# A graph attention layer on one core: the split of the next h moved ahead of the tile's last combine, a simpler row bias, and one more block of each tile transposed on TensorE

## The reference

```python
h = jnp.maximum(_layernorm(x, axis=-1), 0.0)
scores = jnp.einsum('nd,md->nm', h, ks)
scores = jax.nn.leaky_relu(scores, negative_slope=0.2)
scores = jnp.where(adj > 0, scores, NEG_BIG)
attn = jax.nn.softmax(scores, axis=1)
x = x + jnp.einsum('nm,md->nd', attn, ks)
```

## Time and profile before

| | |
|---|---|
| Median of three runs | 1803.49 us |
| The profiled execution | 1804.0 us |
| Its span | 1802.2 us |
| Mean granted TensorE clock | 0.994 |
| TensorE matmul busy | 1617.3 us, 90% |
| ScalarE busy | 1606.0 us, 89% |
| VectorE busy | 1564.4 us, 87% |
| GpSimd busy | 750.0 us, 42% |

### The profile page before, as it was taken

How to read it: one execution, slowest core, us unless ns; L and a number is a source line. 1 busy time by engine, 2 the same in 40 slices (tenths; PEclk the granted TensorE clock), 3 DMA queues, 4 the chain that set the end, 5 groups by cost and what they waited for, 6 DMA issues and landing times. The chain is left out here.

```text
span 1802.2 us, 37484 instructions
## 1 busy us (share of the span) xinstructions
PE 1617.3 (90%) x13442; PEld 1185.6 (66%) x13442; DVE 1564.4 (87%) x2592; ACT 1606.0 (89%) x2081; POOL 750.0 (42%) x713
## 2 busy tenths in 40 slices
PE   5799898898898898898898998988988988989988
PEld 3466666676666676666676666666766666666666
DVE  7888898898888888888888888988988888888885
ACT  7798898898898898898898988988988988989988
POOL 1344344443443443443443443444434434434433
PEclk9899999999999999999999999999999999999999
DMA  7699999999999999999999999999999999999996
GB/s 216 189 241 232 243 237 242 244 230 242 240 237 239 238 241 235 245 239 234 245 232 242 241 234 243 234 237 250 231 242 245 227 245 238 221 246 242 234 246 125
DMA packets 613686, 421.91 MB, mean 234 GB/s; under 512 B 547968, under 2 KB 580736, under 8 KB 580736
## 3 DMA queue, kind: packets, MB, share of 16 engines
q1 hardware_dynamic: 613504, 419.53, 97.7%
HBM read 281.02 MB, written 4.19 MB: 158 GB/s over the span
## 5 line engine op out<-in xcount | busy, mean ns | idle before, releaser
L322 POOL TENSOR_TENSOR halves<-scores,halves 128x512 f16<-128x512 f32 x512 | 596.5, 1165 | 995.0 <-ACT halves L485 995.0
L607 DVE CUSTOM_DVE_ANT_0 scores<-ps_scores,mask,minus_scale 128x1024 f32<-128x1024 f32 x512 | 654.8, 1279 | 3.3 <-PE ps_scores L370 2.7
L468 ACT ACTIVATE scores<-scores,neg_max 128x1024 f32<-128x1024 f32 x512 | 582.3, 1137 | 0.0
L461 ACT ACTIVATE scores<-scores 128x1024 f32<-128x1024 f32 x512 | 537.6, 1050 | 9.8 <-DVE pair_min L607 9.7
L368 PE MATMUL ps_scores<-keysT_hi,hT_hi 128*128 128x512 f16 x1024 | 390.2, 381 | 166.3 <-DVE hT_lo L536 154.1
L616 DVE TENSOR_TENSOR probsT_lo<-ps_T,probsT_hi 128x512 f16<-128x512 f32 x512 | 351.8, 687 | 192.2 <-ACT probsT_hi L476 192.0
L476 ACT ACTIVATE probsT_hi<-ps_T 128x512 f16<-128x512 f32 x512 | 305.6, 597 | 167.5 <-PE ps_T L379 161.9
L394 PE MATMUL ps_out<-keys,probsT_hi 128*128 128x258 f16 x2048 | 399.6, 274 | 6.3 <-issue 4.5
L370 PE MATMUL ps_scores<-keysT_hi,hT_lo 128*128 128x512 f16 x1024 | 390.4, 381 | 0.0
L589 DVE TENSOR_SCALAR mask<-adj_in 128x2048 bf16<-128x2048 int32 x256 | 390.1, 1524 | 0.1
L369 PE MATMUL ps_scores<-keysT_lo,hT_hi 128*128 128x512 f16 x1024 | 390.0, 381 | 0.0
(11 more groups left out here) (52 smaller groups left out, 749.1 us busy)
## 6 DMA issues: line engine op xcount, KB each, us to landing
adj_in<-in_adj_dram SPq DMA_DIRECT2D x256, 1024.0 KB, 5.6
turned<-halves SPq DMA_TRANSPOSE x512, 6.0
x_in<-in_x_dram SPq DMA_DIRECT2D x64, 64.0 KB, 5.3
keys_in<-in_L_gnn_ks_dram SPq DMA_DIRECT2D x8, 512.0 KB, 7.3
x_res<-in_x_dram SPq DMA_DIRECT2D x64, 64.0 KB, 4.9
out_dram<-out_tile SPq DMA_DIRECT2D x64, 64.0 KB, 5.3
```

Source lines behind the costliest of these rows:

```text
L322: nc.gpsimd.tensor_tensor(half[:, BLOCK:2 * BLOCK], probs(t, b), half[:, 0:BLOCK], ALU.subtract) \
L461: nc.scalar.activation(s, s, ACT.Prelu, alpha=1.0 / SLOPE).then_inc(leaky_ready, 1)
L468: nc.scalar.activation(s, s, ACT.Exp, bias=neg_max[:, t % 2:t % 2 + 1], scale=-SLOPE) \
L607: nc.vector.tensor_tensor_reduce(out=score_pair(q, p), in0=ps_scores[:, slots, :].rearrange("p s k -> p (s k)"), in1=mask[:, (p // 2) % 2, ...
```

## The change

There are four edits.

1. `split_h` moves on VectorE from step 15, where it stood behind the last combine and `minimum`, to step 14 ahead of the last combine. So that its input is there, `transpose_h` moves on TensorE from step 13 to step 12, `weigh` and `finish` on VectorE from step 11 to step 10 (there ahead of the combine of pair 5), and the store of the tile and the load of the residual on SyncE from step 13 to step 11.
2. The row bias loses an instruction. Before, an amount of 9.7 was added only where the maximum was small, which took a comparison (L637) and a multiply-add (L643). Now 7.99 is always added.
3. Block 15 leaves `BY_DMA`. Its high half is then made on ScalarE from PSUM in step 3, its low half on VectorE in step 3, it is transposed on TensorE in step 3 and multiplied in step 5. Seven blocks of a tile stay with the DMA.
4. Functions for a variant with the high half on VectorE, which had no blocks, are gone.

```diff
-    BY_DMA = tuple(b for b in range(BLOCKS) if b % 2 == 1)
+    BY_DMA = tuple(b for b in range(BLOCKS) if b % 2 == 1 and b != 15)
...
-    LIFT = 14 * 0.6931471805599453
-    LIFT_BELOW = 2.0 ** 22
+    LIFT = 7.99
...
-                    if j == 13 and prev:
+                    if j == 11 and prev:
                         store(i - 1)
...
-                    if j == 13 and ahead:
+                    if j == 12 and ahead:
                         transpose_h(i + 2, odd)
...
-                nc.vector.tensor_scalar(lift[:, :], plain_max[:, :], plain_max[:, 0:1], LIFT_BELOW ** 2,
-                                        ALU.mult, ALU.is_lt) \
-                    .then_inc(lift_ready, 1)
-                dve.wait_ge(lift_ready, q + 1)
                 if q > 1:
                     dve.wait_ge(probs_ready, (q - 1) * PAIRS)
-                nc.vector.scalar_tensor_tensor(out=neg_max[:, q % 2:q % 2 + 1], in0=lift[:, :], scalar=LIFT,
-                                               in1=plain_max[:, :], op0=ALU.mult, op1=ALU.add) \
+                nc.vector.tensor_scalar(neg_max[:, q % 2:q % 2 + 1], plain_max[:, :], LIFT, None, ALU.add) \
                     .then_inc(neg_max_ready, 1)
...
-                        if j == 15:
+                        if j == 14:
                             split_h(i + 2, odd)
-                    if prev and j == 11:
+                    if prev and j == 10:
                         weigh(i - 1, 1 - odd)
                         finish(i - 1, 1 - odd)
```

More of the change, by code:

```diff
@@ L38, in gat_kernel @@
     HI_LAG = 2
-    HI_DVE_LAG = 3
     LO_LAG = 3
@@ L42, in gat_kernel @@
     ADD_LAG = 10
-    BY_DMA = tuple(b for b in range(BLOCKS) if b % 2 == 1)
+    BY_DMA = tuple(b for b in range(BLOCKS) if b % 2 == 1 and b != 15)
     BY_PE = tuple(b for b in range(BLOCKS) if b not in BY_DMA)
-    HI_ON_DVE = tuple(b for b in BY_DMA if False)
-    HI_ON_ACT = tuple(b for b in BY_DMA if b not in HI_ON_DVE)
     EPS = 1e-5
@@ L109, in gat_kernel @@
         plain_max = sbuf("plain_max", [P, 1], fp32)
-        lift = sbuf("lift", [P, 1], fp32)
         neg_max = sbuf("neg_max", [P, 2], fp32)
@@ L152, in gat_kernel @@
         plain_max_ready = sem("plain_max_ready")
-        lift_ready = sem("lift_ready")
         neg_max_ready = sem("neg_max_ready")
@@ L161, in gat_kernel @@
         half_hi_ready = sem("half_hi_ready")
-        half_hi_dve_ready = sem("half_hi_dve_ready")
         half_lo_ready = sem("half_lo_ready")
@@ L190, in nth_pe @@
             return t * len(BY_PE) + sum(c < b for c in BY_PE)
[L192 to L196, removed]
         def nth_dma(t, b):
@@ L316, in split_half_lo @@
                 n = nth_dma(t, b)
[L317 to L320, removed]
+                pool.wait_ge(half_hi_ready, n + 1)
                 half = halves[:, n % R_SLOTS, :]
@@ L508, in step @@
                         split_keys_hi(j // 2)
-                    split = behind(i, j, HI_LAG, HI_ON_ACT, this, prev)
+                    split = behind(i, j, HI_LAG, BY_DMA, this, prev)
                     if split:
@@ L617, in split_probs_lo @@
                                         ALU.subtract).then_inc(T_lo_ready, 1)
[L619 to L625, removed]
             def minimum(q):
@@ L689, in step @@
                         split_probs_lo(*split)
-                    split = behind(i, j, HI_DVE_LAG, HI_ON_DVE, this, prev)
-                    if split:
-                        split_half_hi(*split)
                     if ahead:
```

## The result

The changed kernel takes 1710.54 us, the median of four runs (1709.86 to 1711.83); the kernel before took 1803.15 beside it. The ratio is 0.9481, with a 95% interval of 0.9463 to 0.9499. The number lies in the predicted range of 1668 to 1720, outside the 1682 to 1702 of the forecast case. One step of the mechanism was wrong: a part of the stop for hT stayed, and the new wait in step 2 did not come.

What follows compares the result with a forecast made beforehand. TensorE's pace inside a tile plus its stop for hT bounds the kernel: 1802.2 - 161.3 (stop) + 27.7 (block 15) + 22.7 (new wait) - 1.0 (end) = 1690.3, plus 1.8 around it: 1692 us; forecast 1682 to 1702, range 1668 to 1720.

Steps and rivals of the forecast that it cites:

- forecast case: The main expectation for the changed kernel: 1692 us, within 1682 to 1702; chance 0.47.
- stop for hT: TensorE waits once per tile, before step 0, for `hT_lo`; removing it was to save 2.56 us a tile.
- new wait in step 2: TensorE would wait in step 2 for `probsT_lo` of block 12; 0.36 us a tile.
- My own loop: Walk through TensorE, ScalarE and VectorE from block 12's output in step 2 back to it; about 25.5 to 25.7 us.
- pairs 6 and 7: Score banks TensorE needs in steps 0 and 2; ready near 20.3 and 23.1, needed at 21.0 and 24.1, so neither decides.
- The loop's size: Tile time of the walked loop, taken as 25.55 us, a wait of 0.36 above TensorE's 25.19.
- held loop: Rival: GpSimd's block 13 meets L633 or the mask, or ScalarE's pair waits add up; 26.0 us a tile, 1718 us; chance 0.22.
- predicted 27.7: Cost in us of block 15's four transposes on TensorE, 0.44 us a tile over 63 tiles.
- The DMAs: Transposes queued behind a 1 MB adjacency load were to keep their margin, 8.0 to 8.8 us; priced at nothing.
- Late turned blocks: Rival: the four blocks behind an adjacency load land late for TensorE; 1843 us at 9.2 us landings; chance 0.03.
- the stop only moved by half: Rival: `transpose_h` in step 12 waits for `finish`, or the first score bank is late; half of 2.56 us returns, 1774 us; chance 0.07.
- no effect: Rival: hT isn't there in time and TensorE's stop stays; 1832 us; chance 0.01.

Runs made afterwards that it cites:

- best: Changed kernel with block 15 back on the DMA, transposing DMAs issued ahead of adjacency loads, and split_h ahead of the low half of block 10; 1640.15 us.
- h_first: Changed kernel with split_h ahead of the low half of block 10 in step 14 instead of behind it; 1691.79 us.
- extra_finish: Changed kernel with one more 128x128 scalar_tensor_tensor into an unused tile in finish, on VectorE; 1726.14 us.
- extra_stats: Changed kernel with one more bn_stats into an unused tile in step 5, on VectorE; 1710.27 us.
- split_only: Kernel before with only the split of h in step 14 and the moves that go with it (edit 1); 1687.76 us.
- after_no15: Changed kernel with block 15 back on the DMA; 1690.50 us.
- turn_first_no15: Changed kernel with block 15 back on the DMA and transposing DMAs issued ahead of the adjacency load of the same step; 1648.26 us.

## Why the prediction was right or wrong

- **The stop for hT and its price.** Right in size: the kernel before had 2.56 us a tile to give, and `best`, with the stop and the late DMAs gone, stands at 24.73 against the predicted 24.75.
- **"In step 14 it runs about two TensorE steps before anyone needs it, so the stop for hT goes."** This is the step that failed. My own loop had TensorE begin step 0 at t = 21.0 and the low half of block 10 start at 20.5 to 20.6; with its 0.69 and the split's 0.54 hT is ready at 21.8, 0.8 behind. I checked pairs 6 and 7 against those times and not hT. 0.56 us of the stop stayed in nearly every tile (the same idle time of 0.40 us stands behind 57 of the 63 waits); `h_first` took it away by moving the split ahead of that low half.
- **The new wait in step 2 for `probsT_lo`.** Wrong, for the same reason: TensorE has already waited in step 0. The loop was the right one up to low half 10 and closes there, through the split, not through the combine, bias and mask. `extra_finish` and `extra_stats` show that it passes through `finish` and not through step 5.
- **The loop's size.** 0.36 us a tile was taken, 0.65 measured (25.84 - 25.19): 63 x 0.29 = 18 us, the difference of 1692 and 1710. That the time still lies in the range is in part luck: the range reached so far up for the held loop, which did not happen.
- **Edit 2.** "Alone it is worth nothing once hT is out of that chain, except in the loop below": in these runs it is worth nothing that can be measured in the loop either, since it isn't in the one that closed.
- **Edit 3.** +0.44 us on TensorE was right only for its work. In the changed kernel block 15 makes the loop longer by 0.98 us (25.82 against the 24.84 of `split_only`), where its transposes and its output, 1.11 us in all, both fall between step 0 and block 2, and it saves late DMAs of about 0.67. The sum, 23 us, is near the predicted 27.7 by accident. "GpSimd and the DMA lose one each" was priced at nothing and was worth some 40 us.
- **The DMAs.** Right for the changed kernel (3.3 us of waiting weight loads), wrong as a margin: at 24.84 us a tile it fails, which made `split_only` miss its 1645 to 1662.
- **The held loop.** Its number, 1718 (1692 + 63 x 0.4 is 1717), is near, but not its cause: L609 has a median of 0.158 us, so GpSimd does not hold it. The walk had the place right, since GpSimd's low half ends just where L609 starts, but the overlap is only 0.02 to 0.04 us in 60 of the 64 tiles, less than L609 lasts anyway. The Trainium skill's rule on the shared ports (SBUF — State Buffer, section Who interferes with whom) makes an instruction with two SBUF inputs wait until GpSimd's has ended. The trace agrees: L609 ends after GpSimd's low half in any case and lasts 0.16 us, where L633 lasted 0.47. In the one tile where they overlap by 0.55, L609 lasts 0.57.
- **Late turned blocks, the stop only moved by half, no effect.** The last two did not happen. Of the first there is a little: six waits of weight loads, 3.3 us, where the rival priced over 100.

The mean tile of the changed kernel is 0.06 us above its median because nine of the last 60 tiles are longer. Six of these nine hold the six waits for turned blocks, and with them 2.5 of the 3.2 us. What made the other three longer stays open, and so does why the output of step 14 starts 0.09 us later with block 15 on TensorE.

## What to carry to other kernels

When a wait is removed, place every remaining input of the waiting instruction on the new timeline, the moved one first: a step earlier in its own engine's program says nothing of when it comes in the other's, where the engines are steps apart. Price work that is added between two points of a closed loop by the loop and not by the engine's total. And read a DMA's margin at the new pace: what stands ahead of it in its queue was worth some 40 us here (`after_no15` against `turn_first_no15`) as soon as the compute no longer hid it.

## What the runs showed of the hardware that was not expected

A stop of TensorE of 2.80 us cost more than itself in about every second tile: behind 31 of the 59 stops of that length the granted clock stood at 0.50 (1.2 GHz) for some 3.5 us, and behind the other 28 it stayed at 1.00 (2.4 GHz). Behind the stops of 2.40 us of the kernel before it stayed at 1.00. Edit 3 alone, 0.44 us of work a tile, so cost 6.1%: about half of it is the longer tile and half the clock.

What GpSimd's low half costs a small VectorE instruction is the time that is left of it, and depends on the instruction. L633 of the kernel before starts 0.46 us before the low half ends and lasts 0.47 in most tiles; with edit 3 alone 0.75 us are left and it lasts 0.77; L609 of the changed kernel has 0.02 to 0.04 us left and lasts 0.16. L606, which has one input and lies wholly beside the low half (1035.16 in the timeline), lasts 0.16 as well.
